# Residual addition and modulation's shift in two halves each, on GpSimd and VectorE, in a 1-core kernel of four conditioned layers

## The reference

```python
# layer 0: graph attention in two directions, 16 heads, 20 keys, masked by the edges, then x + relu(...)
# layers 1 and 3: an attention block and an MLP block; layer 2: two MLP blocks (hidden 128 and 256)
mod = silu(condition) @ Wada + bada                  # shift, scale, gate of each block, one row per sequence
xn = (x - mu) * rsqrt(var + EPS) * g + b             # over the 128 features
xm = xn * (1.0 + scale[:, None, :]) + shift[:, None, :]
x  = x + gate[:, None, :] * (block(xm) + bias)       # block: 16-head attention, or W2 @ gelu(W1 @ xm + b1)
```

## Time and profile before

| | |
|---|---|
| time, median of 3 runs | 567.05 us |
| the profiled execution's own time | 570.62 us |
| its span, first to last instruction | 568.7 us |
| TensorE busy | 476.4 us (84%) |
| VectorE (DVE) busy | 429.7 us (76%) |
| ScalarE (ACT) busy | 383.0 us (67%) |
| GpSimd (POOL) busy | 392.8 us (69%) |
| longest holders in the chain of waits | GpSimd 27%, VectorE 24%, TensorE 24% |

### The profile page before, as it was taken

One profiled execution on the slowest core, in us unless ns is written; L12 is line 12 of the kernel. 1 busy time (PEld: TensorE's weight loads), 2 busy tenths in 40 slices (PEclk: granted clock), 3 DMA queues, 4 the chain that ended last, 5 costly groups with the idle time before them and its releaser, 6 DMA issues.

```text
span 568.7 us, 21089 instructions
## 1 busy us (share of the span) xinstructions
PE 476.4 (84%) x9062; PEld 324.6 (57%) x9062; DVE 429.7 (76%) x914; ACT 383.0 (67%) x633; POOL 392.8 (69%) x408
## 2 busy tenths in 40 slices
PE   5877686898899789888899988767899988887996
PEld 2445354566557566465566555455576665565674
DVE  5888899899728856966899967898995454688841
ACT  7895375657587848666796836745866656686961
POOL 2768666667567879559887848655649899755546
PEclk9989898999599969999999987998999999899999
DMA  8514134123042620451433330212344232153321
GB/s 290 194 42 159 60 85 117 47 77 97 9 106 76 199 82 1 117 147 56 128 100 108 111 86 23 68 39 61 112 122 111 75 82 69 28 139 89 94 78 75
DMA packets 23468, 53.43 MB, mean 94 GB/s; under 512 B 5840, under 2 KB 8144, under 8 KB 23376
## 3 DMA queue, kind: packets, MB, share of 16 engines
q1 hardware_dynamic: 22912, 51.14, 31.5%
q10 hardware_dynamic: 432, 0.94, 0.4%
q0 software_dynamic: 32, 0.01, 0.1%
HBM read 39.74 MB, written 2.88 MB: 75 GB/s over the span
## 4 chain that ended last, share of the span: by engine, by line
POOL 27%; DVE 24%; PE 24%; issue 11%; ACT 6%; DMA 4%; SPq 4%; POOLq 0%; DVEq 0%; ACTq 0%
POOL x L682 5%; PE work L1169 5%; POOL x L678 4%; POOL rstd L672 4%; PE work L1178 4%; POOL xm L689 4%; DVE prob L932 4%; PE work L1128 4%; DVE mx L925 3%; POOL kbd L656 3%; POOL prob L667 2%; SPq L580 2%; PE work L1101 2%; DVE prob L927 2%; PE work L1048 2%
## 5 line engine op out<-in xcount | busy, mean ns | idle before, releaser
L793 ACT ACTIVATE xn<-x,nmr,rstd 128x128 f32<-128x128 f32 x192 | 78.5, 482 | 41.4 <-POOL nmr L675 41.3
L1169 PE MATMUL work<-xm,w_layer 128*128 128x512 f32 x176 | 91.5, 634 | 10.4 <-POOL xm L689 9.7
L1178 PEld LDWEIGHTS work<-w_layer,prob 128*128 128x128 f32 x704 | 83.0, 195 | 12.8 <-ACT prob L798 8.7
L1178 PE MATMUL work<-w_layer,prob 128*128 128x128 f32 x704 | 86.8, 280 | 2.3 <-ACT prob L798 2.2
L798 ACT ACTIVATE prob<-work,first 128x512 f32<-128x512 f32 x88 | 58.7, 684 | 42.7 <-PE work L1169 42.5
L678 POOL TENSOR_TENSOR x<-x,q_gate 128x512 f32<-128x512 f32 x48 | 60.8, 1273 | 31.7 <-DMA q_gate<-gates_out 31.7
L932 DVE STREAM_TRANSPOSE prob<-prob 128x1024 f32<-128x1024 f32 x64 | 78.4, 1232 | 2.5 <-ACT prob L784 2.5
L682 POOL TENSOR_TENSOR x<-x,q_gate 128x512 f32<-128x512 f32 x48 | 60.7, 1271 | 24.1 <-DVE q_gate L971 24.0
L689 POOL TENSOR_TENSOR xm<-turned_in,mod 128x512 f32<-128x512 f32 x48 | 50.6, 1056 | 30.1 <-DVE turned_in L966 30.1
L1128 PE MATMUL work<-vbd,prob 128*32 128x36 f32 x4096 | 52.6, 208 | 21.8 <-issue 10.2
L1128 PEld LDWEIGHTS work<-vbd,prob 128*32 128x32 f32 x4096 | 46.1, 117 | 41.1 <-issue 27.2
(11 more groups left out here) (138 smaller groups left out, 933.9 us busy)
## 6 DMA issues: line engine op xcount, KB each, us to landing
q_gate<-gates_out SPq DMA_DIRECT2D x192, 128.0 KB, 2.9
vbd<-v_ev SPq DMA_DIRECT2D x128, 72.0 KB, 2.4
kbd<-in_adj SPq DMA_DIRECT2D x8, 704.0 KB, 5.0
turned_in<-in_x_tok SPq DMA_DIRECT2D x8, 256.0 KB, 3.0
out_x<-x SPq DMA_DIRECT2D x8, 256.0 KB, 2.2
turned_in<-in_x_feat SPq DMA_DIRECT2D x7, 256.0 KB, 4.5
w_layer<-in_weights SPq DMA_DIRECT2D x2, 768.0 KB, 5.3
w_layer<-in_modw SPq DMA_DIRECT2D x1, 768.0 KB, 7.4
```

What stands on the lines that cost most here:

```text
L793: act.activation(xn[s][:, t], x[s][:, t], ACT.Identity, scale=rstd[s][:, t:t + 1], bias=nmr[s][:, t:t + 1]).then_inc(xn_ready[s], 1)
L1169: pe.matmul(bank(s, f"h{j}.{u}"), w[UP[j]][:, 0, u * D:(u + 1) * D], xm[s][:], start=True, stop=True).then_inc(filled[s], 1)
L1178: last = pe.matmul(bank(s, f"y{a}")[:, t * D:(t + 1) * D], hT[s][u][:, t * P:(t + 1) * P], w[DOWN[a]][:, u], start=(u == 0 and t == 0), st ...
```

## The change

GpSimd's shift and residual add are cut in two by token. `HALF = 2`: GpSimd does tokens 0 and 1 (256 elements per partition), VectorE tokens 2 and 3.

- *modulate*: VectorE multiplies in two pieces of 256 elements and counts `scaled` after each; GpSimd starts its half of the shift after the first. VectorE then waits for its own second piece and adds the shift to its half (a third count of `scaled`). Both halves call `add_shift`, whose line is L495 on both engines. The bank `xn` is free after the second count.
- *project / down*: VectorE counts `y_ready` after the product with the gate (L990), waits for it itself and for `biased`, and adds its half to `x` (L994), a second count. GpSimd adds the other half (L694).
- *stats*: `bn_stats` takes tokens 2 and 3 first, which wait only for VectorE's own add, then tokens 0 and 1, which wait for `x_ready`.
- Whoever needs the whole of `xm` or `x` waits for both counts (`await_xm`, `await_x`).
- All five strings of `MERGE` are new; the stages and who takes part in them are the same.

```diff
--- before.py
+++ after.py
@@ -79,6 +79,7 @@
 ATTN_OF_BLOCK = {0: 2, 4: 3}
 NATT = 4
 UNITS = 4
+HALF = 2
 
 
 def by_pair(kind, a):
@@ -164,24 +165,24 @@
...
 MERGE = {
-    "tensor": ("001020420142012402044200420402042230011321302020103303221113013010120323112032000020123213212130"
...
+    "tensor": ("001020442012042044142020024010402320023123012010203032123013103101013232213102003020301212121201"
...
 }
 ORDERS = {engine: order(engine, merge) for engine, merge in MERGE.items()}
...
@@ -437,6 +438,7 @@
         def await_x(eng, c, j):
             if j:
                 eng.wait_ge(x_ready[c % NS], count(c, NBLK, j))
+                eng.wait_ge(y_ready[c % NS], count(c, 2 * NBLK, 2 * j))
             else:
                 eng.wait_ge(graph_ready[c % NS], count(c, 1, 1))
 
@@ -452,8 +454,8 @@
         for j_, a_ in ATTN_OF_BLOCK.items():
             READ[f"oT a{a_}"] = (oT_ready, 2, a_ - 1)
         for j_ in range(NBLK):
-            READ[f"xn{j_}"] = (scaled, NBLK, j_ + 1)
-            READ[f"y{j_}"] = (y_ready, NBLK, j_ + 1)
+            READ[f"xn{j_}"] = (scaled, 3 * NBLK, 3 * j_ + 2)
+            READ[f"y{j_}"] = (y_ready, 2 * NBLK, 2 * j_ + 1)
             for u_ in range(BLOCKS[j_][2]):
                 READ[f"h{j_}.{u_}"] = (h_ready, NHID, HIDDEN_BEFORE[j_] + u_ + 1)
 
@@ -485,6 +487,16 @@
         def by_head(s, a):
             n = NB * width(a)
             return kbd[s][:, 0:(GRAPH_HEADS if a < 2 else GH) * n].rearrange("p (h n) -> p h n", n=n)
+
+        def add_shift(eng, s, a, c, part):
+            shift = mod[:, 2 * a + 1, c * NB:(c + 1) * NB].rearrange("p (t b) -> p t b", b=BT)
+            turned_out = keys_order(xm[s][:]) if BLOCKS[a][0] == "attn" else as_seqs(xm[s][:])
+            scaled_x = as_seqs(xm0[s][:])[:, part]
+            return eng.tensor_tensor(turned_out[:, part], scaled_x, shift[:, part].unsqueeze(3).broadcast_to(scaled_x.shape), ALU.add)
+
+        def await_xm(eng, c, j):
+            eng.wait_ge(xm_ready[c % NS], count(c, NBLK, j + 1))
+            eng.wait_ge(scaled[c % NS], count(c, 3 * NBLK, 3 * j + 3))
 
         def await_mod(eng, j):
             eng.wait_ge(mod_ready, j + 1)
@@ -585,7 +597,7 @@
                     sp.wait_ge(scored[s], count(c, NATT * PAIRS, NATT * PAIRS))
                     load_adj(c + NS)
                 if kind == "next_x":
-                    sp.wait_ge(xm_ready[s], count(c, NBLK, NBLK))
+                    await_xm(sp, c, NBLK - 1)
                     load_x(c + NS)
                 if kind == "store":
                     await_x(sp, c, NBLK)
@@ -677,17 +689,14 @@
                     pool.wait_ge(gate_loaded[s], count(c, 16 * BT * NBLK, 16 * BT * (a + 1)))
                     pool.tensor_tensor(x[s][:], x[s][:], gate_bias[s], ALU.add).then_inc(biased[s], 1)
                 if kind == "residual":
-                    pool.wait_ge(y_ready[s], count(c, NBLK, a + 1))
+                    pool.wait_ge(y_ready[s], count(c, 2 * NBLK, 2 * a + 1))
                     pool.wait_ge(biased[s], count(c, NBLK, a + 1))
-                    pool.tensor_tensor(x[s][:], x[s][:], qT[s], ALU.add).then_inc(x_ready[s], 1)
+                    pool.tensor_tensor(x[s][:, 0:HALF], x[s][:, 0:HALF], qT[s][:, 0:HALF], ALU.add).then_inc(x_ready[s], 1)
                 if kind == "modulate":
-                    pool.wait_ge(scaled[s], count(c, NBLK, a + 1))
+                    pool.wait_ge(scaled[s], count(c, 3 * NBLK, 3 * a + 1))
                     if c < NS:
                         await_mod(pool, a)
-                    shift = mod[:, 2 * a + 1, c * NB:(c + 1) * NB].rearrange("p (t b) -> p t b", b=BT)
-                    turned_out = keys_order(xm[s][:]) if BLOCKS[a][0] == "attn" else as_seqs(xm[s][:])
-                    pool.tensor_tensor(turned_out, as_seqs(xm0[s][:]), shift.unsqueeze(3).broadcast_to([P, T, BT, S]), ALU.add
-                                       ).then_inc(xm_ready[s], 1)
+                    add_shift(pool, s, a, c, slice(0, HALF)).then_inc(xm_ready[s], 1)
 
             for kind, a, c in ORDERS["gpsimd"]:
                 stage(kind, a, c)
@@ -951,11 +960,17 @@
                     dve.scalar_tensor_tensor(out=x[s][:], in0=o[1][s], scalar=0.0, in1=x_in[s], op0=ALU.max,
                                              op1=ALU.add).then_inc(graph_ready[s], 1)
                 if kind == "stats":
-                    await_x(dve, c, a)
-                    for t in range(T):
+                    tokens = [*range(HALF, T), *range(HALF)]
+                    if a:
+                        chain(y_ready, 2 * NBLK, 2 * a)
+                    else:
+                        await_x(dve, c, a)
+                    for t in tokens:
+                        if a and t == 0:
+                            dve.wait_ge(x_ready[s], count(c, NBLK, a))
                         dve.bn_stats(stats[s][:, t], x[s][:, t]).then_inc(dve_step[s], 1)
-                    for t in range(T):
-                        dve.wait_ge(dve_step[s], count(c, OWN_STEPS, OWN["stats", a] - T + t + 1))
+                    for k, t in enumerate(tokens):
+                        dve.wait_ge(dve_step[s], count(c, OWN_STEPS, OWN["stats", a] - T + k + 1))
                         dve.bn_aggr(mv[s][:, t], stats[s][:, t]).then_inc(dve_step[s], 1)
                     own(("aggr", a))
                     dve.tensor_reduce(neg_mean[s][:], mv[s][:, :, 0:1], AX_X, ALU.add, negate=True).then_inc(mean_ready[s], 1)
@@ -963,13 +978,20 @@
                     await_fill(dve, c, f"xn{a}")
                     if c < NS:
                         await_mod(dve, a)
-                    dve.tensor_tensor(by_seq(xm0[s][:]), by_seq(bank(s, f"xn{a}")), seqs(mod[:, 2 * a], c), ALU.mult
-                                      ).then_inc(scaled[s], 1)
+                    for k in range(2):
+                        part = slice(k * NB // 2, (k + 1) * NB // 2)
+                        dve.tensor_tensor(by_seq(xm0[s][:])[:, part], by_seq(bank(s, f"xn{a}"))[:, part], seqs(mod[:, 2 * a], c)[:, part],
+                                          ALU.mult).then_inc(scaled[s], 1)
+                    chain(scaled, 3 * NBLK, 3 * a + 2)
+                    add_shift(dve, s, a, c, slice(HALF, T)).then_inc(scaled[s], 1)
                 if kind in ("project", "down"):
                     await_fill(dve, c, f"y{a}")
                     dve.wait_ge(gate_loaded[s], count(c, 16 * BT * NBLK, 16 * BT * (a + 1)))
                     dve.tensor_tensor(gate[s], bank(s, f"y{a}").rearrange("p (t f) -> p t f", f=D), gate[s], ALU.mult
                                       ).then_inc(y_ready[s], 1)
+                    chain(y_ready, 2 * NBLK, 2 * a + 1)
+                    dve.wait_ge(biased[s], count(c, NBLK, a + 1))
+                    dve.tensor_tensor(x[s][:, HALF:T], x[s][:, HALF:T], qT[s][:, HALF:T], ALU.add).then_inc(y_ready[s], 1)
 
             for kind, a, c in ORDERS["vector"]:
                 stage(kind, a, c)
@@ -1039,7 +1061,7 @@
                     if a == 0:
                         pe.wait_ge(sf_ready[s], count(c, 2, 1))
                     if a >= 2:
-                        pe.wait_ge(xm_ready[s], count(c, NBLK, 1 if a == 2 else 5))
+                        await_xm(pe, c, 0 if a == 2 else 4)
                     if c < NS and a == 0:
                         pe.wait_ge(graph_loaded, 16)
                     if c < NS and a >= 2:
@@ -1161,7 +1183,7 @@
                         await_bank(pe, c, f"h{j}.{u}")
                         keep_warm(bank(s, f"h{j}.{u}"), "hidden")
                     if u == 0:
-                        pe.wait_ge(xm_ready[s], count(c, NBLK, j + 1))
+                        await_xm(pe, c, j)
                         if c < NS and j == 2:
                             pe.wait_ge(w_loaded[2], 16)
                     if u or not WARM.get("hidden"):
```

34 lines of the change are left out of this document (17 added, 17 removed).

## The result

The changed kernel takes 590.77 us (median of 4 runs, 586.79 to 593.42), the kernel before 567.08: ratio 1.0393, 95% interval 1.035 to 1.0436. It is slower by 24 us where 8 were forecast: the right side, inside the range, and three times the size. The ratio is formed from the single runs and is not the quotient of the two medians; by it the loss is 22 us.

A forecast was written before the change was run, and what follows sets the result against it. Four nearly equally loaded engines, bound by whichever queue a stretch waits on. Saving, VectorE's price and GpSimd's waits: -21 + 20 + 4 = +3 to -21 + 26 + 4 = +9 us, taken +8: 575.0 us, range 556 to 592.

The forecast's parts named there:

- GpSimd's saving: GpSimd's halved residual adds and shifts: 48 us less busy time, counted on the chain as 21 us gained.
- VectorE's own 46 us: VectorE's new work without waits: product cut in two and two half-size adds, 0.96 us per block over 48 blocks.
- the waits, both engines: VectorE waiting 37 us inside its adds for GpSimd's operations, and GpSimd some 15 us for VectorE's, priced at 4 us.
- Charged at its present share of the chain, 24%: Price of VectorE's 83 us of new time: 20 us at 24%, or 26 us at the 31.8% of a VectorE-ruled stretch.
- the lean to +8: Choice near the high price's +9 us over the low price's +3, since VectorE takes over in the block stretches.
- 83 us on VectorE: VectorE's whole new time: 46 us of its own work plus 37 us of waiting for GpSimd.
- GpSimd's 4: GpSimd's waits for VectorE's adds, some 15 us, charged at 27% of the chain as 4 us.
- In the other 34 and 29 it was still at something else: GpSimd busy before 34 of 48 residual adds and 29 of 48 shifts, so VectorE's adds wait some 0.6 us.
- means of 0.7 to 0.9: Test in the profile after: VectorE's residual add and shift half average 0.7 to 0.9 us instead of 0.40.
- 88 to 91% busy: Test in the profile after: VectorE's busy share, with GpSimd at 60 to 64%.
- The page's full block: Blocked VectorE adds cost their full 0.40 us after GpSimd's release: 10 us more on VectorE, 2 more in the sum.
- Side by side: Rival: VectorE's and GpSimd's halves run together, only 46 us of own work new, 557 us; chance 0.30.

The follow-up runs named there:

- e1: The changed code with all five MERGE strings of the kernel before, against the kernel before: 586.05 us, ratio 1.0327.
- g1: The kernel before with GpSimd's residual add and shift on tokens 0 and 1 only, nobody doing the others: 552.37 us, ratio 0.9689.
- g2: The kernel before with GpSimd's adds on tokens 0 and 1 only, plus 96 statistics instructions for nobody on VectorE: 565.72 us, ratio 1.0001.

## Why the prediction was right in its sign and wrong in its size

The steps of the change by ratio (each against the kernel before, not measured against each other): before 1, saving alone 0.9689, with floating VectorE time 1.0001, with the time in the adds 1.0018, the exclusion 1.0273 (e1: 1.0327), the new orders 1.0393.

| step | forecast, us | measured, us |
|---|---|---|
| GpSimd's saving | -21 | -17.6 |
| VectorE's own 46 us | +11 to +15 | +17.7 floating, +18.7 in the adds |
| the waits, both engines | +13 to +16 | +14.5 to +17.5 |
| the new orders | 0 | +3.7, not clear of noise |
| sum | +3 to +9, taken +8 | +22 |

- **What held of the mechanism.** Two-input adds wait for GpSimd's operation and need 0.28 us after it; GpSimd's residual half came to 0.903 (forecast 0.9), GpSimd to 61% (60 to 64), and VectorE leads GpSimd in the chain. The bias was rarely late, as taken (2.7 us, 3 times).
- **The saving** was sized nearly right from the chain, 17.6 for 21 us. So was VectorE's time added alone, 0.21 where 0.24 was charged. The chain shares of before were good for each edit by itself.
- **The failed step is "Charged at its present share of the chain, 24%"**, with 31.8% as the dear end. The saving and the price were added as if each stood alone, and they interact. The same 96 instructions cost 1.2% without the saving and 3.1% beside it, 11 us apart (give or take 7): 0.61 us for each us of VectorE's busy time. The whole of the halves shows the same: from g1 to e1 VectorE's busy time rises by 58.7 us (427.4 to 486.1) and the ratio by 0.0638, 36 us, GpSimd's waits included, which is 0.62 for each. No share in a chain would have given that, neither VectorE's before (24%) nor its share in g1 (22%), in g2 (32%) or in the change (35%). What fits is that VectorE's time, once GpSimd is light, takes up the slack that the saving made; that the price doubles and more is shown, this reading of it is argued.
- **Of the 14 us that the forecast lacks** (22 for 8), against its own high end, VectorE's own time has 4, the waits 2, the saving 3, the orders 4, and the lean to +8 instead of +9 the last one.
- **The amount was wrong the other way, which hid part of this.** The forecast put 83 us on VectorE, and it got 58.5. At 24 to 31.8% these would have made 14 to 19 us, with GpSimd's 4 at most 23, where e1 paid 36 for the like amount. Most of the missing time is waits: 19 us on VectorE for 37. "In the other 34 and 29 it was still at something else" did not carry over to the residual: VectorE was to stand in 34 of the 48 residual adds and stood in 10, and GpSimd's halves waited instead (median 0.962 for 0.728). The product in two pieces also cost less than its two rows said, 35.8 us for 32.5, 3 more where 8 were charged, since the pieces overlap. Two errors cancelled in the waits' term, and that the measured time lies inside the range is in part luck. The forecast's tests "means of 0.7 to 0.9" and "88 to 91% busy" failed for the same reason (0.558, 0.693; 83%).
- **The page's full block** (the Trainium skill, "SBUF — State Buffer", "Who interferes with whom") against the rows' 0.12 us less: the trace decides for the rows, 0.28 us after the release at both places shown, where the add alone takes 0.424.
- **The new orders** were taken as neutral; they cost 0 to 6 us. I had read how they move VectorE's and GpSimd's instructions and not what they do to ScalarE's functions.
- **Side by side**: it could not be, but without the exclusion it would not have gained either: 1.0018.

The waits that answer to the earlier trace rows: GpSimd had more idle time in front of both halves (24.0 and 30.1 us before). Together that is 33.5 us more, the size of what its busy time fell by (34.0).

```profile
POOL x L694 <- DVE q_gate L990: 44.9, 23, 7.9
...
POOL xm L495 <- DVE turned_in L983: 42.7, 25, 4.0
```
